# Layer 3's recurrence beside layer 2's expert blocks: the two sums of the numerator made by DMA transfers that add, where GpSimd added them

## The reference, cut to what matters

```python
ek = exp(minimum(k, 30)); ekv = ek * v          # k = v = fside in every layer
a = a * decay + ekv_t;  b = b * decay + ek_t     # forward: nf, df; reversed: nb, db
euk = exp(minimum(u + k, 30))
num = nf + nb - ekv + euk * v
den = df + db - ek + euk
out = sigmoid(r) * (num / maximum(den, 1e-8)) * (0.8 + 0.2 * tf)   # r = x of the layer
```

## Time and profile before

| | us |
|---|---|
| median of 3 runs | 1744.48 (1742.62 to 1749.67) |
| the profiled execution: its time | 1747.82 |
| its span, first to last instruction | 1746.0 |
| first to last PE matmul of the expert blocks | 889 to 1119 |
| one turn of five blocks and two units | 29.04 |
| PE without work between the last expert block and the first product of layer 3 | 12.6 |

### The profile page before, as it was taken

The page is one execution under the profiler, slowest core; times in us unless marked ns, Lnnn a source line. Parts: engine busy times, 40 slices in busy tenths (PEclk is TensorE's granted clock), DMA queues, the critical chain, the costliest instruction groups (busy, mean ns, idle before and its releaser), DMA issues.

```text
span 1746.0 us, 19673 instructions
## 1 busy us (share of the span) xinstructions
PE 1506.8 (86%) x6413; PEld 967.7 (55%) x6446; DVE 1115.2 (64%) x1773; ACT 968.5 (55%) x1266; POOL 377.9 (22%) x299
## 2 busy tenths in 40 slices
PE   5666578789995899996469999689999999999997
PEld 2222234444442466664334545378888888888886
DVE  7899588899996889994728787854322222222222
ACT  6765588889993789985237777743321221221210
POOL 0000011111210111110613233551231321321311
PEclk9999798999997999998779999899999999999998
DMA  7864632312102877763955454570110100100001
GB/s 282 278 218 165 231 125 90 103 61 73 61 31 77 230 199 184 184 155 102 398 176 189 139 187 139 185 266 20 37 36 1 36 28 9 37 21 17 1 24 72
DMA packets 107718, 212.38 MB, mean 122 GB/s; under 512 B 12260, under 2 KB 29156, under 8 KB 103908
## 3 DMA queue, kind: packets, MB, share of 16 engines
q1 hardware_dynamic: 95012, 180.72, 30.6%
q0 software_dynamic: 12032, 29.37, 7.1%
q10 hardware_dynamic: 576, 1.05, 0.2%
HBM read 139.79 MB, written 58.72 MB: 114 GB/s over the span
## 4 chain that ended last, share of the span: by engine, by line
PE 45%; POOL 2%; DVE 2%; issue 2%; DMA 1%; ACT 1%; SPq 0%; DVEq 0%; POOLq 0%; ACTq 0%
PE ffn_po L2477 10%; PE ffn_pg L2458 10%; PE ffn_pu L2458 10%; PE moe_psum L1889 7%; PE moe_psum L1910 3%; PE ffn_po L1584 2%; POOL tokens_by_slot L2094 1%; PE ffn_po L1571 1%; PE moe_psum L1877 1%; PE moe_psum L1845 1%; DVE x L2547 1%; PE moe_psum L1900 0%; POOL up_front L1554 0%; DVE x L1617 0%; DMA tokens_by_slot<-moe_zrow,rt_slot 0%
## 5 line engine op out<-in xcount | busy, mean ns | idle before, releaser
L2380 ACT ACTIVATE up_front<-ffn_pg,ffn_gate_chunk 128x512 f32<-128x512 f32 x64 | 44.1, 689 | 320.7 <-PE ffn_pg L2458 271.7
L2537 DVE SCALAR_TENSOR_TENSOR up_front<-ffn_pu,ffn_up_scale,up_front 128x512 f32<-128x512 f32 x64 | 48.0, 750 | 231.6 <-PE ffn_pu L2458 231.5
L2547 DVE SCALAR_TENSOR_TENSOR x<-ffn_po,ffn_out_scale,x 128x512 f32<-128x512 f32 x128 | 87.2, 744 | 149.7 <-PE ffn_po L2477 149.7
L2431 POOL TENSOR_TENSOR ffn_hl<-up_front,ffn_hh 128x512 fp32r<-128x512 f32 x64 | 82.8, 1295 | 396.6 <-ACT ffn_hh L2387 396.6
L942 POOL TENSOR_TENSOR l_rr<-l_rr,constants 128x1 f32<-128x1 f32 x32 | 28.9, 902 | 483.7 <-DVE l_rr L969 483.7
L2477 PE MATMUL ffn_po<-ffn_hh,ffn_wh 128*128 128x512 f32 x256 | 102.0, 398 | 4.2 <-DVE x L2547 2.9
L2458 PE MATMUL ffn_pg<-zhi,ffn_wh 128*128 128x512 f32 x256 | 101.5, 396 | 0.5
L2477 PE MATMUL ffn_po<-ffn_hh,ffn_wl 128*128 128x512 f32 x256 | 101.1, 395 | 0.0
L2477 PE MATMUL ffn_po<-ffn_hl,ffn_wh 128*128 128x512 f32 x256 | 100.8, 394 | 0.0
L2458 PE MATMUL ffn_pu<-zhi,ffn_wh 128*128 128x512 f32 x256 | 100.8, 394 | 0.0
L2458 PE MATMUL ffn_pg<-zhi,ffn_wl 128*128 128x512 f32 x256 | 100.4, 392 | 0.0
(11 more groups left out here) (345 smaller groups left out, 3985.4 us busy)
## 6 DMA issues: line engine op xcount, KB each, us to landing
wkv_k<-in_fside SPq DMA_DIRECT2D x64, 256.0 KB, 4.2
ratio<-wkv_fn SPq DMA_DIRECT2D x64, 256.0 KB, 2.3
wkv_ek<-exp_k SPq DMA_DIRECT2D x48, 256.0 KB, 3.0
wkv_ekv<-exp_k_times_v SPq DMA_DIRECT2D x48, 256.0 KB, 3.7
moe_zt<-tokens_by_slot SPq DMA_DIRECT2D x39, 256.0 KB, 3.0
expert_out<-moe_eo SPq DMA_DIRECT2D x39, 256.0 KB, 2.2
up_front<-in_gated SPq DMA_DIRECT2D x8, 1024.0 KB, 5.1
x<-in_x SPq DMA_DIRECT2D x4, 1024.0 KB, 6.8
```

The source lines that it names most:

```text
L2380: eng.activation(hf[t], p_g[t][:, :], ACT.Silu, scale=scale).then_inc(*E(f"silu{t}").inc)
L2431: eng.tensor_tensor(hl[t][slot % 2][:, :], hf[t], hh[t][slot % 2][:, :].bitcast(F32), ALU.subtract).then_inc(*E(f"hl{t}").inc)
L2537: eng.scalar_tensor_tensor(hf[t], p_u[t][:, :], scale, hf[t], ALU.mult, ALU.mult).then_inc(*E(f"h{t}").inc)
L2547: last = eng.scalar_tensor_tensor(x[:, o, :], p_o[:, o, :], out_s[:, o:o + 1], x[:, o, :], ALU.mult, ALU.add)
```

## The change

Layer 3's `Wkv` gets `added=("later", "num")`. POOL's two additions for a unit, `num_u` (`fn += k`) and `num_later` (`fn += bn`), are gone. In their place POOL issues two transfers from SBUF to SBUF that add: `add_later_n` (`fn += bn`) once the backward scan is done, and, when that has landed, `add_now_n` (`fn += k`). Their order on POOL's list changes too. Whatever waited for `num_u` or `num` now waits for the landing of the second transfer: `load_k` of the unit two later, the backward `scan_n` of the unit two later, and `quotient`.

```diff
@@ scan_alone, load_k
             if i >= self.slots:
-                eng.wait_ge(*self.E("both" if values == "scan_d" else "num").at(i - self.slots))
+                eng.wait_ge(*(self.E("both").at(i - self.slots) if values == "scan_d" else self.done("num", i - self.slots)))
...
-    def num_u(self, eng, i, p):
-        eng.wait_ge(*self.E("scan_n_forward").at(i))
-        eng.wait_ge(*self.E("euv").at(i))
-        fn = self.fn[p][:, :]
-        eng.tensor_tensor(fn, fn, self.k[p][:, :], ALU.add).then_inc(*self.E("num_u").inc)
-
-    def num_later(self, eng, i, p):
-        eng.wait_ge(*self.E("scan_n").at(i))
-        eng.wait_ge(*self.E("num_u").at(i))
-        fn = self.fn[p][:, :]
-        eng.tensor_tensor(fn, fn, self.bn[p][:, :], ALU.add).then_inc(*self.E("num").inc)
-
     def load_k(self, eng, i, p):
         if i >= self.slots:
-            eng.wait_ge(*self.E("num_u").at(i - self.slots))
+            eng.wait_ge(*self.done("num", i - self.slots))
@@ experts
-            w = Wkv(core, r, c, d, ratio3, 3, 2, preloads=("recip",))
+            w = Wkv(core, r, c, d, ratio3, 3, 2, preloads=("recip",), added=("later", "num"))
@@ experts, gpsimd
             for j in range(TURNS + 0):
                 for u in unit(j, 0, 0):
                     w.products(eng, u, u % w.slots)
+                for u in unit(j, 0, 0):
+                    w.add_later_n(eng, u, u % w.slots)
                 for u in unit(j, 0, 1):
                     w.products(eng, u, u % w.slots)
                 for u in unit(j, 0, 0):
-                    w.num_u(eng, u, u % w.slots)
-                for u in unit(j, 0, 0):
-                    w.num_later(eng, u, u % w.slots)
+                    w.add_now_n(eng, u, u % w.slots)
                 for u in unit(j, 0, 1):
-                    w.num_u(eng, u, u % w.slots)
+                    w.add_later_n(eng, u, u % w.slots)
                 for u in unit(j, 0, 1):
-                    w.num_later(eng, u, u % w.slots)
+                    w.add_now_n(eng, u, u % w.slots)
```

## The result

| | before | after |
|---|---|---|
| median, us | 1746.28 (1741.87 to 1751.38, 20 runs) | 1752.43 (1748.55 to 1757.26, 20 runs) |
| ratio after/before, 95% interval | | 1.0036 (1.0027 to 1.0045) |
| profiled execution: time, span, us | 1747.82, 1746.0 | 1749.32, 1747.5 |

The changed kernel is 0.0036 x 1746.28 = 6.3 us slower, with an interval from 4.7 to 7.9. This is inside the 0.5% called "no change", as forecast, but the forecast said +2.0, and its own range ended at +5.5 (1750 on its level of 1744.5). The end of this part shows where 2.9 us of that come from.

What follows compares the result with a forecast made beforehand. The prediction took PE to bound the stage, busy 228.3 of 230.3 us. Turns 0 and end +2.0 gave 1749.8 on the profiled execution's terms, 1746.5 on the 1744.5 median's level, with a range from 1743.5 to 1750 (66%).

Steps and rivals of the forecast that it cites:

- No change: Whole kernel: the forecast lies within 0.5%, 8.7 us, which a measurement cannot tell from no change.
- Turns, forecast 0: Turns of the expert blocks: B's sum lands at 957.4 to 958.2, so PE loses nothing, 0 us.
- last harmless time of 958.5: In the turn followed: PE loses nothing if B's sum lands by 957.5 + 1.0, before `hidden` of block 1 comes late.
- that of layer 2's middle turns: Turns: DMA load taken as equal to layer 2's, so its median landings, 5.4 us for `bn` and 3.9 for `k`.
- the turns lose: Rival, 17%: B's two landings exceed 10.4 us together, and the excess reaches PE through `hidden` in about seven turns; 1772.
- misread pair: Layer 2's transfers from 602, landing in 7.1 and 6.8 us, taken as one pair, a minority of 2 of 15.
- End, forecast +2.0, bounds -0.6 and +4.8: End of the last turn: layer 3's first gather issued 1.5 us later, plus 0.5 for the queue; +2.0.
- the 0.5 for the queue: End: gathers stand behind the last sum's 256 KB in POOL's queue, 1.64 us at most, 0.5 of it taken.
- What was taken away, forecast 0: POOL's 32 additions gone: some 5 us of DVE time a turn, worth nothing in the sum.
- DVE's time reaches the end: Rival, 5%: DVE's savings reach PE at the stage's edges, at most 2.0 us inside and 0.6 at the end; 1741.9.
- The hidden end: Rival, 12%: transfers land in 3.3 us each and gathers start when the last result is stored; -0.6, 1743.9.
- The list of what would show it: Signs expected in the profile after, on PE, DVE, landings, `quotient`'s wait, the first gather and PE's gap.

Runs made afterwards that it cites:

- number 3: Changed kernel with each unit's transfers swapped, k added first, bn second, A's pair ahead of B's product; 1747.09 us, ratio 1.0007 to the kernel before.
- number 8: Changed kernel with only the even units (A) by adding transfers, the odd ones (B) by GpSimd's additions; 1755.34 us, ratio 0.9999 to the kernel before.
- number 1: Changed kernel with the last turn's units 14 and 15 back on GpSimd's additions; 1750.66 us, ratio 1.0028 to the kernel before.
- number 5: Changed kernel with the last turn's units on GpSimd and `hidden` of block 1 ahead of B's `quotient`; 1745.82 us, ratio 1.0004 to the kernel before.
- number 2: Kernel before with only the last turn's units 14 and 15 by adding transfers; 1746.91 us, ratio 1.0012 to the kernel before.
- number 6: Changed kernel with k added first in units 0 to 13 and units 14 and 15 on GpSimd's additions; 1746.86 us, ratio 1.0003 to the kernel before.
- Number 4: Changed kernel, all units by DMA, with `hidden` of block 1 ahead of B's `quotient` on DVE's list; 1750.51 us, ratio 1.0034 to the kernel before.
- number 12: Changed kernel with only A by DMA, B by GpSimd, and DVE's `first_low` behind the second batch's diagonals; 1742.72 us, ratio 0.9981 to the kernel before.
- number 10: Kernel before with DVE's subtraction `first_low` moved behind the second batch's diagonals; 1755.62 us, ratio 0.9998 to the kernel before.

## Why the prediction was right in kind and short by four microseconds

"No change" held, and the end's mechanism with it. For the turns this was luck: the forecast said that they lose nothing, and they lose the larger part. It stayed inside the 8.7 us called no change because 0.5 us a turn is little, not because the turns were read rightly. On the forecast's own level the result is 1744.5 x 1.0036 = 1750.8, above the 1750 at which its range ended.

*Turns, forecast 0: this is the step that failed.* The landing was put at 957.4 to 958.2 against a last harmless time of 958.5. The chain came out at +15.0 of B's product, where +14.5 was free and +13.4 to +14.2 was forecast. Piece by piece: the backward scan ends 0.3 late, because `both` kept its 1.70; 0.3 goes from there to the issue, where I had nothing; the first landing takes 4.8 (forecast 5.4); 0.3 to the next issue (0.2); the second landing takes 5.4 (3.9 to 4.7). So the size of the second landing was the largest error. It came from taking the stage's load for "that of layer 2's middle turns". The DMA share during four of layer 2's second transfers that landed in 3.9 us was 0.83 to 0.86; here, with the adding transfers on top of the 0.85 and 0.79 of the earlier trace rows, it is 1.08 and 1.05. That the share is why is argued, not shown: in number 3 the second landing took 4.9 at 1.08. Number 3 shows that the lateness of the pair is the cause (started 2.2 us earlier, the pair costs nothing), number 8 that it comes with B's pair, and numbers 1 and 5 the way through `hidden`. The cost is 4.9 us (3.1 to 6.6) over seven turns.

The rival *the turns lose* had this mechanism and this way, and the sign of being wrong that the prediction named, PE waiting for `hidden` of block 1, is what came. The rival's threshold of 10.4 us for the two landings was too high by the 0.7 us of the other pieces: above 9.7 the pair costs, and its 10.2 cost 0.5 a turn. Its price of 1772 needed landings of 7.1 and 6.8, which no turn had. Its chance was judged from a misread pair: the 6.8 and the 7.1 of layer 2 are the second transfer of one unit and the first of the next. Taken unit by unit, 4 of layer 2's 16 pairs took over 10.4 us together (14.8, 12.1, 14.6 and 11.0), not 2 of 15. The prediction's 1759 for 1.5 us a turn is also 1 to 2 us more than its own terms give (1744.5 + 10.5 + 2.0, or + 3 at the end).

*End, forecast +2.0, bounds -0.6 and +4.8.* The mechanism was right and the sum within what number 2 measured, +2.1; the changed kernel's trace has 3.4. The term that was mis-sized is the first gather's: +3.55 in place of +1.5. Its parts: the first transfer is issued 1.08 behind PE's last matmul and not 0.17 (the forward scan took 1.88 beside POOL's product, behind a wait of 0.97 for a store), which is 0.9; the first landing and the step to the second issue took 6.72 and not 5.6, which is 1.1. How much of the 0.5 for the queue came true can't be separated.

*What was taken away, forecast 0*: right. 25 us of DVE time in 170 are gone, and PE's turn is no shorter; number 6 has most of that saving (22 us) with both losses mended, and is no faster than the kernel before. So the rival *DVE's time reaches the end* did not come. By the Trainium skill, "SBUF — State Buffer", section "Who interferes with whom", a DVE instruction with two SBUF inputs contends with a GpSimd instruction that reads SBUF. The trace agrees: without POOL's additions DVE works 17.16 us of 27 in place of 22.19, and `both`, which still runs beside POOL's product, still takes 1.70.

*The hidden end* did not come: the landing that the gathers wait for, put at 3.3 there, took 6.4. The figure of the Trainium skill, "DMA: Bandwidth & Descriptors", section "Anatomy of one DMA — SWDGE (gpsimd) path" (an estimate of 2.6 us for 256 KB), was below every adding transfer here; the least took 3.2.

*The list of what would show it.* Right: PE 27 of 27, the scan at 1.2, DVE 5 us less, landings of 4 to 6 (3.5 to 5.9 in the turns), PE's gap 14 to 16 (14.37). Wrong: `both` at 0.7 (1.70), `quotient` waiting under 1 us (1.3 to 2.0), the first gather within 3 us (+3.55). The wait of `quotient` is the loss, and "PE 27 of 27" did not see it.

**Open.** Number 4's time (+5.9 where its trace and number 5 say some +2). Why the second landing takes 5.4. Which half of number 12 gives its 3 us. How often the half clock at the end comes, of which each profile shows one draw.

## What to carry to other kernels

Two serial transfers in place of two additions took 10.5 us here from the first issue to the sum (951.71 + 5.4 - 946.60), where GpSimd's two additions for a unit took 3.8 (1120.64 to 1124.48 in the last turn of the kernel before). Before doing it, read which wait stands on the in-order list behind them, and what PE needs from further down that list. Then add first the operand that is ready first: the landings still follow each other, but the pair starts earlier, here by 2.2 us, which was enough in the turns. Keep such transfers from standing ahead of gathers that PE waits for. A window of "27.00 of 27.00" is no proof against a loss of 0.4 a turn: time one and the same instruction near the start and near the end of the stage in both kernels, or a marked instruction over several turns.

## What the runs showed of the hardware that was not expected

The issue of an indirect gather on POOL takes 0.94 to 1.6 us, but 3.0 to 4.1 when it starts while DVE's subtraction of 128x3072 with two inputs in SBUF (3.35 us) is running. In number 10 it moved with that instruction. Whenever it starts, it ends 0.8 us behind the subtraction (1134.37 and 1133.55 before, 1138.89 and 1138.06 after), while the issue that began 0.01 us ahead of the subtraction in the changed kernel took its usual 0.96. DVE's forward scan and POOL's product overlap in the last turn, and the one that started second was the longer: before, the scan started first and took 1.23, the product 2.10; after, the product started first and took 1.27, the scan 1.88. The granted clock behind one and the same wait of 2.91 us was 0.50 for 6 us in one execution and 1.00 in another, which moved a span by 2.9 us.
